# The mean taken from the aggregate in GpSimd's streaming operation, and the key norm's sums begun at D times epsilon

## The reference, cut to what matters

```python
def _layernorm(x, axis=-1, eps=1e-05):
    m = jnp.mean(x, axis=axis, keepdims=True)
    v = jnp.var(x, axis=axis, keepdims=True)
    return (x - m) / jnp.sqrt(v + eps)

x = x + tanh(g_xattn[0]) * L0_xattn(_layernorm(x), ctx)   # teacher attention
x = x + tanh(g_ffn[0])   * L0_ffn(_layernorm(x))          # ternary weights, int8 activations
x = x + tanh(g_xattn[1]) * L1_xattn(_layernorm(x), ctx)   # 16 heads, rmsnorm on q and k
x = x + tanh(g_ffn[1])   * L1_ffn(_layernorm(x))          # 64 experts, top 8, plus a shared one

def rmsnorm(x, g, eps=1e-05):                             # in L1_xattn
    var = jnp.mean(jnp.square(x), axis=-1, keepdims=True)
    return x * jax.lax.rsqrt(var + eps) * g
scores = jnp.einsum('bqhd,bkhd->bhqk', rmsnorm(q, gq), rmsnorm(k, gk)) * D ** -0.5
```

## Time and profile before

| | before |
| --- | --- |
| median of 3 runs | 615.6 us (615.5 to 615.78) |
| the profiled execution's own time | 616.09 us |
| its span in the profile | 614.3 us |
| PE busy | 603.3 us (98%) |
| DVE busy | 477.9 us (78%) |
| ACT busy | 422.7 us (69%) |
| POOL busy | 236.7 us (39%) |
| granted clock of PE | 1.00 |

### The profile page before, as it was taken

One profiled execution on the slowest core, in us unless ns is written; L12 is line 12 of the kernel. 1 busy time (PEld: TensorE's weight loads), 2 busy tenths in 40 slices (PEclk: granted clock), 3 DMA queues, 4 the chain that ended last, 5 costly groups with the idle time before them and its releaser, 6 DMA issues.

```text
span 614.3 us, 11619 instructions
## 1 busy us (share of the span) xinstructions
PE 603.3 (98%) x3644; PEld 522.6 (85%) x3644; DVE 477.9 (78%) x1139; ACT 422.7 (69%) x1082; POOL 236.7 (39%) x282
## 2 busy tenths in 40 slices
PE   8979999999999999999999999999999999999997
PEld 6757899999999999999998888888887888887886
DVE  3999988987777787688876787788777676777776
ACT  6999999888888888889897344465444444443442
POOL 5999998576665566656662020000000000000000
PEclk9999999999999999999999999999999999999999
DMA  8513202000000000000030545453856466545640
GB/s 299 196 53 102 95 11 78 2 2 2 2 2 2 1 2 2 1 2 1 11 121 3 170 147 154 129 171 96 216 156 167 116 176 175 156 154 149 195 128 34
DMA packets 33653, 56.47 MB, mean 92 GB/s; under 512 B 12800, under 2 KB 13504, under 8 KB 33600
## 3 DMA queue, kind: packets, MB, share of 16 engines
q1 hardware_dynamic: 33312, 55.82, 30.4%
q10 hardware_dynamic: 288, 0.00, 0.0%
HBM read 53.45 MB, written 1.31 MB: 89 GB/s over the span
## 4 chain that ended last, share of the span: by engine, by line
PE 89%; DVE 5%; ACT 4%; issue 1%; POOL 1%; DVEq 0%; ACTq 0%; POOLq 0%
PE bank L310 25%; PE bank L312 25%; PE bank L311 25%; PE bank L985 4%; PE bank L960 2%; PE bank L952 2%; DVE hs L2088 1%; PE bank L912 1%; PE bank L1026 1%; PE bank L829 1%; DVE attT_lo L2182 1%; PE bank L835 1%; ACT att L1575 1%; ACT w L1478 1%; PE bank L815 1%
## 5 line engine op out<-in xcount | busy, mean ns | idle before, releaser
L1623 ACT ACTIVATE inter_hi<-inter 128x512 fp32r<-128x512 f32 x63 | 39.8, 632 | 140.5 <-DVE inter L2287 140.5
L310 PE MATMUL bank<-xnT_hi,front_hi 128*128 128x512 f32 (+1 forms) x260 | 102.0, 392 | 0.0
L312 PE MATMUL bank<-xnT_hi,front_lo 128*128 128x512 f32 (+1 forms) x260 | 101.7, 391 | 0.0
L311 PE MATMUL bank<-xnT_lo,front_hi 128*128 128x512 f32 (+1 forms) x260 | 101.6, 391 | 0.0
L2291 DVE TENSOR_TENSOR inter_lo<-inter,inter_hi 128x512 fp32r<-128x512 f32 x63 | 43.6, 692 | 37.9 <-ACT inter_hi L1623 37.3
L1575 ACT ACTIVATE att<-bank,shift,rq 128x256 f32<-128x256 f32 x128 | 71.3, 572 | 0.0
L596 POOL TENSOR_TENSOR att<-att,rowinv 128x512 f32<-128x512 f32 x60 | 63.1, 1067 | 11.1 <-DVE rowinv L2187 11.1
L2260 DVE TENSOR_TENSOR prod<-gate_s,bank 128x512 f32<-128x512 f32 x63 | 43.3, 687 | 21.6 <-PE bank L312 19.5
L2170 DVE TENSOR_REDUCE rowmax<-bank 128x2 f32<-128x512 f32 x64 | 43.6, 686 | 20.7 <-PE bank L312 20.4
L311 PEld LDWEIGHTS bank<-xnT_lo,front_hi 128*128 128x128 f32 x260 | 48.9, 188 | 11.3
L312 PEld LDWEIGHTS bank<-xnT_hi,front_lo 128*128 128x128 f32 x260 | 48.8, 188 | 11.3
(11 more groups left out here) (273 smaller groups left out, 1811.7 us busy)
## 6 DMA issues: line engine op xcount, KB each, us to landing
w_all<-w_rows SPq DMA_DIRECT2D x128, 128.0 KB, 3.0
raw<-in_expert_w SPq DMA_DIRECT2D x32, 384.0 KB, 3.5
wvo_raw<-in_expert_w SPq DMA_DIRECT2D x16, 384.0 KB, 3.5
e_more<-in_expert_w SPq DMA_DIRECT2D x16, 384.0 KB, 3.6
raw<-in_head_qk SPq DMA_DIRECT2D x8, 384.0 KB, 3.1
wvo_raw<-in_head_vo SPq DMA_DIRECT2D x4, 384.0 KB, 3.8
w_keep<-in_head_vo SPq DMA_DIRECT2D x4, 384.0 KB, 3.3
gate_raw<-in_gate_wT SPq DMA_DIRECT2D x2, 704.0 KB, 9.0
```

Source lines behind the costliest of these rows:

```text
L310: pe.matmul(out, l_hi, r_hi_, start=start, stop=False, skip_group_check=True)
L311: pe.matmul(out, l_hi, r_lo_, start=False, stop=False, skip_group_check=True)
L312: return pe.matmul(out, l_lo, r_hi_, start=False, stop=stop, skip_group_check=True)
L1623: act.activation(inter_hi[:, slot, :], inter[:, slot, :], ACT.Copy).then_inc(a_Ihi, 1)
```

## The change

GpSimd no longer makes the negated copy of the means (eight instructions, four at L476 and four at L508). Its normalising operation subtracts `mv[:, i, 0:1]` in place of adding `negm[:, i:i + 1]`.

The four key sums of groups 2 to 31 begin at D times epsilon in place of 0, so that each holds D times what `msq` held. The instruction that wrote `msq[:, 4:8]` for these groups (30 in all), with two waits ahead of it, goes; `rms_k` takes the power from the sums themselves, and waits for the last of them. The power is smaller by D ** -0.5, so that factor is taken out of `gk`. `mean_k(n)` has a wait for `g_rk` at n - 1 ahead of its sums, which `ssq`'s two slots need. The first two groups keep their instruction, with other constants.

```diff
             def root_0(b):
                 pool.wait_ge(v_pw1, b + 1)
-                pool.tensor_scalar(negm[:, c], mv[:, c, 0], -1.0, 0.0, ALU.mult, ALU.add)
                 pool.tensor_scalar(vare[:, c], mv[:, c, 1], 1.0, EPS, ALU.mult, ALU.add).then_inc(g_va0, 1)
             def root_3(b):
                 pool.wait_ge(v_pw1, b + BATCH + 1)
-                pool.tensor_scalar(negm[:, c], mv[:, c, 0], -1.0, 0.0, ALU.mult, ALU.add)
                 pool.tensor_scalar(vare[:, c], mv[:, c, 1], 1.0, EPS, ALU.mult, ALU.add).then_inc(g_va0, 1)
             def normalise_0(i):            # normalise_1 the same
-                pool.tensor_scalar(u[:, i, :], x[:, i, :], negm[:, i:i + 1], rstd[:, i:i + 1], ALU.add,
+                pool.tensor_scalar(u[:, i, :], x[:, i, :], mv[:, i, 0:1], rstd[:, i:i + 1], ALU.subtract,
                                    ALU.mult).then_inc(g_u0, 1)
             def rms_k(n):
-                pool.wait_ge(v_mk, n + 1)
+                if n < 2:
+                    pool.wait_ge(v_mk, n + 1)
+                else:
+                    pool.wait_ge(v_sqK, n * 4 - 4)
                 wait(pool, g_kn, n)
-                pool.tensor_tensor(rk[:, :], msq[:, 4:8], minus_half[:, 0:4], ALU.pow).then_inc(g_rk, 1)
+                sums = msq[:, 4:8] if n < 2 else ssq[:, n % 2, 4:8]
+                pool.tensor_tensor(rk[:, :], sums, minus_half[:, 0:4], ALU.pow).then_inc(g_rk, 1)
             def first_mean_k(n):
-                dve.tensor_scalar(msq[:, 4:8], ssq[:, n % 2, 4:8], 1.0 / D, EPS, ALU.mult, ALU.add).then_inc(v_mk, 1)
+                dve.tensor_scalar(msq[:, 4:8], ssq[:, n % 2, 4:8], 1.0, D * EPS, ALU.mult, ALU.add).then_inc(v_mk, 1)
             def mean_k(n):
                 dve.wait_ge(a_rawK, n + 1)
                 wait(dve, v_sqK, n * 4 - 8)
-                wait(dve, v_mk, n - 1)
+                wait(dve, g_rk, n - 1)
                 for c in range(4):
-                    dve.tensor_tensor_reduce(out=k_sq[:, c // 2, c % 2, :], in0=k, in1=k, scale=1.0, scalar=0.0,
+                    dve.tensor_tensor_reduce(out=k_sq[:, c // 2, c % 2, :], in0=k, in1=k, scale=1.0, scalar=D * EPS,
...
-                wait(dve, g_rk, n)
-                dve.wait_ge(v_sqK, n * 4 - 4)
-                dve.tensor_scalar(msq[:, 4:8], ssq[:, n % 2, 4:8], 1.0 / D, EPS, ALU.mult, ALU.add).then_inc(v_mk, 1)
             def key_gain():
-                dve.tensor_scalar(gk[:, :], gqk_raw[:, 0:1], gqk_raw[:, 1:2], float(D) ** -0.5, ALU.mult,
+                dve.tensor_scalar(gk[:, :], gqk_raw[:, 0:1], gqk_raw[:, 1:2], 1.0, ALU.mult,
                                   ALU.mult).then_inc(v_gk, 1)
```

More of the change, by code:

```diff
@@ L93, in flamingo_kernel @@
         sc2 = sb("sc2", [P, TILES])
-        negm = sb("negm", [P, TILES])
         sumh = sb("sumh", [P, TILES])
```

## The result

The changed kernel takes 623.82 us (median of 4 runs, 623.51 to 625.97) against 615.55 for the kernel before beside it: a ratio of 1.0139, 95% interval 1.0126 to 1.0152. I had forecast 615.1, in a range of 613.8 to 616.6. The profiled execution took 623.86 us, with a span of 622.1.

What follows compares the result with a forecast made beforehand. TensorE, busy 603.3 of 614.3 us, was taken as the bound. Gains 0.10 + 0.22 + 0.20 = 0.52 us took the span from 614.30 to 613.78, and the median from 615.6 to 615.1 us; range 613.8 to 616.6.

Steps and rivals of the forecast that it cites:

- the one on the subtract: GpSimd's normalising tiles: subtract costs the same as add, 0.55 us for an undisturbed 256-column tile, so a cost of 0.
- the upper of the two bounds: Normalising tile with each function at GpSimd's two-input rate, 2.4 ns an element: 1.2 us, 0.65 more a tile.
- The slow rival: Subtract slow on GpSimd, 0.65 a tile: 0.2 + 1.8 at the first norm, 1.0 at 54.83; 618.2 us, chance 0.09.
- the cover between 57 and 110 us: TensorE busy 53.00 of 53.00 us there, so the three copies in that window were counted as covered.
- The negated copies: Eight GpSimd copies removed, 0.26 us each, 2.1 in all; only 0.10 reaches TensorE, at the transposes of 54.83.
- msq and the earlier power: Key norm: rk starts 0.27 us earlier, DVE 0.2 a group; TensorE gains 0.22 at 136.78 and 0.20 at 319.19.
- The moved wait: mean_k(n) waits ahead of its sums for rms_k(n - 2), one group looser than before: cost 0.
- the start value: Key sums begin at D x EPS, a constant in instructions already there: cost 0.
- the constants: Gain without D^-0.5, and other constants for the first two groups' msq: cost 0.
- The port of DVE and GpSimd: Earlier rk beside mean_q's msq: taken as 0; under an exclusive lock msq could lose 1.0 us in each of 23 groups.
- unlucky order ahead of 57 us: DVE and GpSimd ordered badly there, one undisturbed tile of 0.55 late: 616.0 us, a bound of the forecast itself.

Runs made afterwards that it cites:

- gp_quiet: Kernel before with single GpSimd operations on scratch data put ahead of its work, VectorE waiting; over 256 columns add-multiply took 554 ns, subtract-multiply 1224; kernel time without meaning.
- copy_sub: Kernel before with the mean copied by 1.0 instead of -1.0 and all sixteen normalising tiles subtracting it instead of adding: 625.87 us, ratio 1.0171.
- sub_first: Kernel before with only the first norm's eight tiles subtracting a positive copy of the mean: 621.49 us against 615.57, ratio 1.0091.
- sub_third: Kernel before with only the third norm's eight tiles subtracting a positive copy of the mean: 619.28 us against 615.57, ratio 1.006.
- copy_zero: Kernel before without its eight negated copies, tiles adding a value from memory set to 0 by one memset: 615.39 us against 615.75, ratio 0.9997.
- no_copy: Kernel before without its eight negated copies, tiles adding a constant 0 instead of the negated mean: 616.77 us against 615.57, ratio 1.0019.
- tok_only: Kernel before with the token norm's part alone: no negated copies, tiles subtract the aggregated mean, key norm unchanged; 623.57 us against 615.43, ratio 1.0128.

## Why the prediction was wrong, point by point

**The step that failed** is the one on the subtract: "The function doesn't matter. I take 0." The measured price is 0.67 us a tile (1224 against 554 ns), the upper of the two bounds that I had set (0.65). The rows I went by were two-input operations. Their 2.4 ns a column hold for any of the three functions, as `gp_quiet` shows too, and say nothing on the scalar operation with one input, which runs at 0.83 with add and multiply and at 3.33 with subtract. It isn't that the second input hides the slow function: over 256 columns the two-input subtract takes 612 ns, half of the 1224 of the scalar one. The two forms have prices of their own for the same function, and a row of one is no evidence for the other. The upper bound rested on the same rows, and came out right by luck (2 x 2.4 = 4.8 ns a column taken for the whole operation; measured are 3.33 ns a column and 0.37 us fixed, which meet it near 256 columns alone). The row nearest in kind,'s rounding with one input, has no subtract; so nothing in the trace excluded the price, and 0.09 was too small a chance for it.

**The slow rival's size** failed as well. It had the right mechanism, at 618.2 in place of 623.8. It let 3.0 us arrive. The kernel that changes the function alone loses 10.4, nearly the 16 x 0.67 = 10.7 of GpSimd's stream. Three things were missing in it. First, the path at 24 us: I looked at the rounded weights and ScalarE, but the power behind them (L491) is what DVE and then TensorE wait for; the first norm's tiles alone cost 5.9 us, not 2.0. The pair at 53 us costs 1.8 and not 1.0, as above. Second, the cover between 57 and 110 us: "53.00 us of TensorE work in 53.00" says that TensorE never waits as things are, not how far its feeder is from making it wait. GpSimd had 47.84 us of work in those 53, and the tiles that stood at 87 and 93 us add 2.0 to the lateness with the third norm's tiles alone. Third, TensorE's clock: the wait of 1.7 us was followed by 3.4 us at the lower level, and by about 1.5 more of lateness at 58 us.

In the kernel after the growth of the lateness divides like this: 2.3 us at the wait of 24 us, 1.8 up to the wait of 57, 1.5 in the stretch of low clock, 0.8 from there to 85 us, 1.1 at the tiles of 88.6 (by the old time) and 0.7 behind. In the profiled runs of `copy_sub` and `sub_first` the low clock comes behind the wait of 24 us instead (3.4 us, 1.7 and 1.3 of lateness), and in that of `sub_third` there is none: its 3.7 us are waits alone. So that 10.4 lies so near the 10.7 of GpSimd's stream is partly chance: some of that stream's time is covered, and the clock adds some. The parts aren't additive to the last tenth (5.9 + 3.7 = 9.6 of 10.4), and what remains I have not separated.

**The negated copies**: 0.10 us forecast. With fast tiles `copy_zero` shows -0.4 in the medians, and an interval that holds 0 and 0.10. As forecast, the gain can't be told from nothing. With slow tiles they are worth about 2 (2.3 between medians), so the value of a GpSimd operation here is not a constant: it is next to nothing while another engine comes last, and near the whole when GpSimd does.

**msq and the earlier power**: 0.22 + 0.20 forecast, 0.47 measured between the medians, both waits seen to go, the power 0.08 behind the last read, 5.0 us of DVE's time saved (I had counted 6), 4.9 of it in the steady loop, and nothing of that reaching TensorE. These steps were right, down to the places. The moved wait, the start value (the sums take a mean of 284 ns, before 289) and the constants cost nothing that shows.

**The port of DVE and GpSimd**: I took 0, by a row in which a small DVE operation ran within a power of GpSimd. That holds for such a pair, and the steady loop stayed full. It doesn't hold for other pairs. In `no_copy` a DVE scalar operation with one input from SBUF and one output to it was held for 1.5 us. In `tok_only` the same one, at 34.06 us, took 1.24 in place of 0.32, beside GpSimd's multiply of 33.46. This is the "unlucky order ahead of 57 us" that I had bounded at 616.0, 0.9 us above the forecast; one such meeting holds the operation for up to 1.5 us, and made `no_copy` 1.2 slower. It is no part of the changed kernel's profiled 8.3, where none of these operations is held. The Trainium skill ("SBUF — State Buffer", Who interferes with whom) names the DVE's `tensor_scalar` in its two-port modes among those that take the shared pair, and says that whoever issues first has it for the whole instruction while the other blocks. By that rule the hold would last to the end of GpSimd's multiply: the trace agrees (31.06, and DVE's end at 31.22).

**A version that beats both**: the key norm's part alone, 614.96 us, is the fastest measured with the whole computation, by 0.1% and with an interval that reaches to no change.

## What to carry to other kernels

Before an operation's function is changed on GpSimd, look for a row of the same form (scalar operation or two-input) with the same function; the other form has another price. A negated copy of a few columns that lets the long operation add in place of subtract is cheap: 0.26 us of the stream for two tiles, against 0.67 for each. And a full TensorE in a window is cover only as deep as the slack of whoever feeds it, which one reads from the feeder's idle time ahead of the slower operation and not from TensorE's. Even the sum of that idle time can deceive: GpSimd had 5.2 us of it in the 53, and of the 4.0 us (6 x 0.67) that six slower tiles cost there, 2.0 reached TensorE.

## What the runs showed of the hardware

- On GpSimd a one-input fp32 scalar operation with two functions costs 0.83 ns a column with add and multiply in either order, over 0.34 us fixed, and 3.33 ns with a subtract or a max in it, over 0.37; subtract as the second function costs the same (`gp_quiet`). Two-input add, subtract and multiply take 0.61 us each over 256 columns.
- DVE's scalar operation over 256 columns in SBUF (0.32 to 0.35 us) took 1.87 us in `no_copy`, where GpSimd's two-input multiply started 0.02 us behind its shown start, so the engine whose start is shown first isn't always the one that goes first.
- Behind TensorE's wait at 57 to 59 us the granted clock was 0.85 over the next two microseconds and 0.53 over the three after them, so a part of a wait's cost lies behind it, where TensorE is shown as busy. The length of the wait alone doesn't say whether this happens: it followed a wait of 2.25 us at 25 us in `tok_only`, and not the one of 2.59 in the kernel after.
